# Layer-norm source tiles taken from a resident buffer, and the squares moved from VectorE to ScalarE, in an AdaLN attention and MoE layer on 8 cores

## The reference

```python
mod = (_silu(L0_c) @ L0_wmod).reshape(4, 6, 1, -1)
sa, ca, ga, sb, cb, gb = (mod[:, 0], ..., mod[:, 5])
ga = (2 * (ga >= 0) - 1) * jnp.maximum(jnp.abs(ga), 0.25)   # gb the same
h = _layernorm(x, axis=-1) * (1 + ca) + sa        # x is (4, 2048, 2048)
x = x + ga * attention(h)                         # 16 heads of 128, causal
h = _layernorm(x, axis=-1) * (1 + cb) + sb
x = x + gb * moe(h)                               # 8 experts top 2, one shared
```

## Time and profile before

| | us |
|---|---|
| median of 2 runs | 4139.27 (4135.47 to 4143.06) |
| profiled execution, its own time | 4139.3 |
| span of its slowest core, core 4 | 4137.7 |
| spans of the other cores | 4119.7 to 4132.9 |
| PE busy (core 4) | 3338.9, 81% of the span |
| DVE busy | 1175.2, 28% |
| ACT busy | 596.3, 14% |

### The profile page before, as it was taken

How to read it: one execution, slowest core, us unless ns; L and a number is a source line. 1 busy time by engine, 2 the same in 40 slices (tenths; PEclk the granted TensorE clock), 3 DMA queues, 4 the chain that set the end, 5 groups by cost and what they waited for, 6 DMA issues and landing times. The chain is left out here.

```text
span 4137.7 us, 46112 instructions; the slowest of 8 cores (4119.7 to 4137.7 us)
## 1 busy us (share of the span) xinstructions
PE 3338.9 (81%) x14133; PEld 1368.3 (33%) x14394; DVE 1175.2 (28%) x2063; ACT 596.3 (14%) x1288; POOL 469.5 (11%) x891
## 2 busy tenths in 40 slices
PE   3434388888888878888895289999999999999997
PEld 0222222222222222222233134444444444444443
DVE  0255522222222222222225612132221222212212
ACT  0122222222222222222201200000000000000000
POOL 1101000000000000000000012122122121211211
PEclk9666677777777777777787589999999999999998
DMA  9866511111111111111122035545555454554544
GB/s 206 145 139 143 114 19 16 18 19 17 20 16 16 16 21 16 16 16 16 16 42 35 1 53 86 77 71 77 74 75 81 68 79 70 74 82 69 74 74 117
DMA packets 128926, 246.51 MB, mean 60 GB/s; under 512 B 15681, under 2 KB 56770, under 8 KB 126402
## 3 DMA queue, kind: packets, MB, share of 16 engines
q0 software_dynamic: 125824, 209.92, 33.3%
q1 hardware_dynamic: 2882, 33.63, 2.3%
HBM read 444.94 MB, written 8.39 MB: 110 GB/s over the span
## 5 line engine op out<-in xcount | busy, mean ns | idle before, releaser
L593 PE MATMUL pacc<-h_full,rA 128*128 128x512 bf16 x2497 | 596.9, 395 | 20.7 <-DMA rA<-wk 14.7
L1298 PE MATMUL pdn<-ysb,rD 128*128 128x512 bf16 x2510 | 565.9, 386 | 15.9 <-DVE ysb L1242 11.5
L1188 PE MATMUL px<-h,rA 128*128 128x512 bf16 x2508 | 564.8, 380 | 3.9 <-ACT comb L347 1.2
L1213 PE MATMUL px<-h,rA 128*128 128x512 bf16 x2508 | 562.2, 379 | 2.7
L593 PEld LDWEIGHTS pacc<-h_full,rA 128*128 128x128 bf16 x2560 | 257.1, 101 | 346.4 <-issue 74.9
L1230 DVE TENSOR_TENSOR ysb<-x1s,px 128x1024 bf16<-128x1024 bf16 x80 | 97.7, 1221 | 960.7 <-PE px L1213 960.7
L1298 PEld LDWEIGHTS pdn<-ysb,rD 128*128 128x128 bf16 x2560 | 253.4, 99 | 327.0 <-issue 36.0
L1188 PEld LDWEIGHTS px<-h,rA 128*128 128x128 bf16 x2560 | 251.1, 98 | 305.1 <-issue 4.8
L1213 PEld LDWEIGHTS px<-h,rA 128*128 128x128 bf16 x2560 | 250.4, 98 | 302.1
L1308 DVE SCALAR_TENSOR_TENSOR x_own<-pdn,gbcl,x_own 128x512 f32<-128x512 f32 x320 | 240.2, 751 | 342.0 <-PE pdn L1298 342.0
L1202 ACT ACTIVATE x1s<-px 128x1024 bf16<-128x1024 f32 x80 | 81.8, 1023 | 1479.5 <-PE px L1188 1479.5
(11 more groups left out here) (153 smaller groups left out, 2433.3 us busy)
## 6 DMA issues: line engine op xcount, KB each, us to landing
rB<-wmodA POOLq DMA_DIRECT2D x96, 512.0 KB, 10.6
rA<-wg POOLq DMA_DIRECT2D x128, 256.0 KB, 4.8
rA<-wu POOLq DMA_DIRECT2D x128, 256.0 KB, 5.2
rD<-wd POOLq DMA_DIRECT2D x256, 128.0 KB, 5.5
xl<-ximg SPq DMA_DIRECT2D x16, 1024.0 KB, 10.1
rA<-wk POOLq DMA_DIRECT2D x32, 256.0 KB, 5.0
rA<-wq POOLq DMA_DIRECT2D x32, 256.0 KB, 4.8
rA<-wv POOLq DMA_DIRECT2D x32, 256.0 KB, 4.8
```

The costliest lines, as they stand in the source:

```text
L593: t.matmul(pacc[:, bank * 512:bank * 512 + 512], ub[:, (dc % 8) * 128:(dc % 8) * 128 + 128], moving_fn(dc, qtr), start=(dc == 0), stop=(dc ...
L1188: lambda t, ub=ub, dc=dc, half=half: t.matmul(px1[:, half * 512:half * 512 + 512], ub[:, (dc % 8) * 128:(dc % 8) * 128 + 128], h2[:, dc * ...
L1213: lambda t, ub=ub, dc=dc, half=half: t.matmul(px3[:, half * 512:half * 512 + 512], ub[:, (dc % 8) * 128:(dc % 8) * 128 + 128], h2[:, dc * ...
L1298: t.matmul(pdn[rot][:, :], ub[:, dloc * 128:dloc * 128 + 128], ysb[:, hc * 1024 + th * 512: hc * 1024 + th * 512 + 512], start=(hc == 0), ...
```

## The change

Two edits are in the diff. First, `emit_ln_cast` makes both bf16 copies on ACT, the second as an activation with `Square`; DVE's multiply and its mark `sq_mark` go. As both norms use this helper, it holds for all 16 + 8 pieces. Second, in LN1 pieces with even `s` take their source from `x_own`; only the eight odd chunks are loaded into `xl`. The two tiles `xl` alternate over the odd pieces alone, and `ld_x(s + 2)` is issued at the head of odd piece `s`, waiting for `v_h` of piece `s - 2`. Even pieces wait for `s_xo`, the landing of `x_own`. Lines behind the helper lie five lower than before up to the loader (L421 is L416, L437 is L432).

```diff
-        s_c1 = em.op("scalar", lambda s: s.activation(xbfb[:, :], x_src_ap, AF.Copy),
-                     waits=w_cast, inc=True)
-
-        def _sq(v):
-            with nc.allow_low_precision(reason="bf16 x^2 operand for LN variance stats"):
-                return v.tensor_tensor(xsqb[:, :], x_src_ap, x_src_ap, ALU.mult)
-        v_sq = em.op("vector", _sq, waits=list(w_cast), inc=True)
-        em.drain("vector")
-        state["cast_mark"] = s_c1
-        state["sq_mark"] = v_sq
+        em.op("scalar", lambda s: s.activation(xbfb[:, :], x_src_ap, AF.Copy),
+              waits=w_cast, inc=True)
+        s_c2 = em.op("scalar", lambda s: s.activation(xsqb[:, :], x_src_ap, AF.Square),
+                     inc=True)
+        state["cast_mark"] = s_c2
...
-        w_mm = [state["cast_mark"], state["sq_mark"], misc["CG"]]
+        w_mm = [state["cast_mark"], misc["CG"]]
...
-        slot = s_idx % 2
+        slot = (s_idx // 2) % 2
...
+    x_wait = [None] * TC
+
+    def src_of(s):
+        if s % 2 == 0:
+            return x_own[:, (s // 2) * 2048:(s // 2 + 1) * 2048]
+        return xl[(s // 2) % 2][:, :]
+
     if SUB1 >= 2:
-        xw0 = ld_x(0)
-        emit_ln_cast(xl[0][:, :], xbf[:, :], xsq[:, :], ln1_state,
-                     extra_waits=[xw0])
+        x_wait[1] = ld_x(1)
+        emit_ln_cast(src_of(0), xbf[:, :], xsq[:, :], ln1_state,
+                     extra_waits=[(s_xo, 16)])
     for s_idx in (range(TC) if SUB1 >= 2 else range(0)):
-        slot = s_idx % 2
+        if s_idx % 2 == 1 and s_idx + 2 < TC:
+            x_wait[s_idx + 2] = ld_x(s_idx + 2)
         pc = None
         if s_idx + 1 < TC:
-            xw = ld_x(s_idx + 1)
-            nslot = (s_idx + 1) % 2
-            pc = (lambda xw=xw, nslot=nslot:
-                  emit_ln_cast(xl[nslot][:, :], xbf[:, :], xsq[:, :],
-                               ln1_state, extra_waits=[xw]))
+            nxt = s_idx + 1
+            ew = [(s_xo, 16)] if nxt % 2 == 0 else [x_wait[nxt]]
+            pc = (lambda nxt=nxt, ew=ew:
+                  emit_ln_cast(src_of(nxt), xbf[:, :], xsq[:, :],
+                               ln1_state, extra_waits=ew))
...
-        x_free[slot] = v_h
+        if s_idx % 2 == 1:
+            x_free[(s_idx // 2) % 2] = v_h
```

More of the change, by code:

```diff
@@ L538, in build_nc @@
                   emit_mod_half(mbh // 2, mbh % 2, ringB, pma_h, p_mt[:, :], stage="b"))
-        v_h = emit_ln_piece(xl[slot][:, :], dst, ca1, 0, p_rs[0:1, 0:128],
+        v_h = emit_ln_piece(src_of(s_idx), dst, ca1, 0, p_rs[0:1, 0:128],
                             p_rq[0:1, 0:128], ln1_state, rows_b1, p_bc1[:, :],
```

## The result

| | before | after |
|---|---|---|
| forecast | | 4077, range 4058 to 4102 |
| time | 4139.27 | 4078.9 to 4085.6 |
| ratio to before | | 0.9853 (0.9821 to 0.9884) |
| profiled execution, slowest core | 4137.7 (core 4) | 4084.0 (core 1) |
| LN1, 15 periods, all cores | 323.8 to 336.2 | 258.5 to 258.7 |

The median over all twelve executions after, 4192.66 us, mixes in seven in which a die ran at a lower clock; only the others are compared. The ratio times 4139.27 is 4078.4 us. The means of the executions compared are 4082.7 us after and 4139.1 before, 56 us apart; the ratio comes out lower since it counts one execution of the kernel before that took 4171.6. "LN1" in the table is DVE's first row instruction (L395 before, L390 after) from the first to the last piece, "attention" from the end of LN1 to the start of the third block.

The account below looks back on a forecast made before the run. ACT's wait for late chunks of x was taken to set LN1's pace. LN1 gains 103.8 - 27.2 - 0.9 = 75.7 us, LN2 loses 13.6: 62.1 off 4139.3 gives 4077.2, range 4058 to 4102.

Parts of the forecast that it names:

- Loads, LN1: First layer norm: with resident even chunks and early odd loads no cast waits; gain 102.5 us plus 1.3, 103.8 us.
- Squares, LN1: First layer norm: Square on ACT adds 1.81 us in each of 15 precasts, 27.2 us, plus 0.9 in the first piece.
- Squares, LN2: Second layer norm: only cost, 7 precasts at 1.81 us, 12.7, plus 0.9 for the first; 13.6 us lost.
- Sum: Whole kernel, core 4: 75.7 gained in LN1 less 13.6 lost in LN2, 62.1 us off 4139.3, giving 4077.2.
- the clock term of my range: Attention: a 0.01 shift of TensorE's granted clock, 0.76, moves 1405.7 us of matmul by up to 18 us.
- What is late next: LN1 after the change: DVE stays last in each piece; the statistics on PE end 3.7 us ahead of L395.
- The modulation units: Rival, LN1: units take the place of x and hold the loop, 4085 to 4154 us; chance 0.10.
- The rule on moving work: Both norms: DVE idle while ACT is on the path, so loads alone would be about 41 us better.
- its own opening point: LN1: a late load of chunk s+1 holds up chunk s through ACT's list; ACT waits 102.5 us, 14 times.

Follow-up runs that it names:

- e1: Changed kernel with the squares back on VectorE, so only the loads differ from the kernel before: 4039.6 and 4044.8 us, ratio 0.9779.
- e2: Kernel before with both copies on ScalarE, loads as before: 4172.6 to 4175.1 us, ratio 1.0098.
- e4: Changed kernel with the square on ScalarE, but behind the copy of rows_b: 4038.4 and 4044.1 us.
- e11: Kernel before, loads unchanged, cast on ScalarE moved behind everything the piece needs, square in its old place on VectorE: 4125.2 us beside 4135.1.
- e5: Kernel before, loads unchanged, both copies on ScalarE at the end of its list of the piece: 4037.6 to 4045.9 us, ratio 0.9773.
- e12: Kernel before with one more wait on POOL, holding back the modulation units until the next chunk's tile is free: 4078.2 and 4080.1 us, ratio 0.9844.
- e8: Changed kernel; LN1: square on VectorE, cast on ScalarE behind rows_b; LN2: both on ScalarE behind rows_b: 4024.3 to 4025.5 us, ratio 0.9735.

## Why the prediction was right, and where it was not

*Loads, LN1* was right. The wait of 102.5 us is gone entirely; from 15 periods of 336.2 us, 103.8 off and 27.2 on, I had 259.6 for core 4, and every core measured 258.5 to 258.7. Core 4 was the end of a range: the gain of LN1 was 77.5 us on it and 65.3 to 77.2 on the others, which had waited less. Attention's first matmul on core 4 starts 79.3 us earlier; I had 76.

*Squares, LN1* was right: 1.89 us, a pitch of 1.80 to 1.81, no table load beyond the one that was there. The run with loads alone (e1) puts the whole cost of the squares at about 40 us against 41.7. What the Trainium skill states (ScalarE: Activation LUTs, "What ACT_TABLE_LOAD costs") held for Square: by it 1.89 us and a pitch of 1.80, in this trace 1.89 and 1.80 to 1.81.

*Squares, LN2*: 7 periods grew by 12.6 us (12.7 expected), and the stretch from the start of the third block to the first matmul of the gating from 127.7 to 140.9, 13.2 against 13.6.

*Sum*: core 4 gained 77.5 us in LN1 and lost 12.6 in LN2; but its span fell by 80.1, since its attention was 10.1 us shorter and its first piece began 1.9 earlier (76.9 of the 80.1). Core 1's span fell by 45.0: LN1 77.2 gained, LN2 12.6 lost, attention 10.6 longer, and 9 more in stretches that nothing in the change reaches. The slowest core of an execution is set by this spread as well, and what was gained in all, 61 us by the ratio and 56 by the means, stands between the two. So the two norms came out as summed (64.9 us off on core 4, 62.1 forecast), and that the time did too is in part luck. Attention varied by 16 us between cores of the execution after, with no part of the change in it. On core 4 it is the clock term of my range: it had 1394.7 us of matmul there at a granted clock of 0.77, where before it had 1405.7 at 0.76, for the same 5237 matmuls in the record. What set the clock was not tried.

*What is late next* held in the changed kernel; DVE is last in each piece, and L390 waits for ACT only in the first, where there is no piece before it.

*The modulation units* was the weak step. I took their DMA work as today's 14.6 us a piece less half a load of x, and forecast a share of 0.75. It is 0.85, which is 0.85 x 240.4 / 14 = 14.6 us a piece; the load that went was made up by slower units. The saturated price of 3.25 a unit, which gave 14.9, was the better number. It did no harm at a period of 17.2, where L266 waited for `rB` 0.2 to 17.0 us by core in the whole of LN1 and LN1 took 258.5 to 258.7 on all of them, and it set the pace as soon as the square was off the chain.

*The rule on moving work.* The Trainium skill (Perfetto Trace Analysis, "Optimizing Scalar/DVE Operations") says that offloading to ScalarE may make sense if VectorE is saturated. I stretched this to say that an idle VectorE should keep its work, and in LN2 it was not even idle, with 102.8 us busy of 128. e1 and e2 (+0.98%) seem to bear the stretched rule out, but it is the place in the list and not the engine that decided. LN2 shows it: 104.1 us before, 116.7 with the square ahead of `rows_b` on ScalarE, 104.1 with it behind (e4), 99.8 with the cast alone behind (e11), 98.8 with both behind (e5).

What my account missed is its own opening point. I wrote that a late chunk s+1 holds up chunk s because its cast stands in front in ACT's list (DVE's list holds it as well, e11), and then costed only the cure by earlier loads. e5 shows the other, and e12 a third: 10.0 us of landing were not the load's own, but partly the price of being issued behind two or three units. The forecast was right since the change makes the landing time irrelevant (10.5 to 13.3 us in the median by core, and no wait), not since I understood it.

## What to carry to other kernels

A wait for a load has three cures, and the timeline tells them apart: issue the load earlier, issue it ahead of the bulk traffic that shares the DMA engines, or move its first consumer behind the work of the present step, in every engine's list that has it. The second was one wait here and gained as much as the change under study (ratios 0.9844 and 0.9853), though less than its loads without its squares (0.9779). Before moving an elementwise copy to another engine, ask what stands behind it in that engine's list: 1.8 us in front of `rows_b` cost 1.8 us a piece, behind it nothing (e1 and e4 agree in both norms within 3 us).

## What the runs showed of the hardware that was not expected

- A 1 MB chunk landed in 10.0 us (median) when two or three units of 1 MB read each had been pushed ahead of it, the first by 1.3 to 2.5 us, at a DMA share of 0.64. In the changed kernel, at a share of 0.85, with two ahead of it, the first by 1.4 to 1.5 us, it took 13.3 (core 1). With the units held back by one wait it landed in 6.1; issued 1.5 to 2.6 us ahead of them, but with the DMA share at 1.00, in 7.1 (e5). The issues of e12, 0.47 us apart, and the saturated stretch of e5:

```profile
280.79 0.33 SPq L511 DMA_DIRECT2D xl<-ximg  x1
```

```profile
281.26 2.18 POOL L101 DMA_DIRECT2D rB<-wmodA  x4 [16.18 <-DVE rowb L396]
```

```profile
175.00:375.00 200.00, 106.78 (x639) 65.23 (x639) 130.49 (x266) 87.34 (x163) 25.32 (x48) 0.71 1.00 194
```

- That stretch shows 194 GB/s, against 162 and 164 in the saturated stretch of units alone. This is not more speed: the column counts bytes as they land, and a unit reads twice what it lands (32 units of 0.52 MB in 104 us are 161 GB/s). By bytes read the two are alike, 323 GB/s for units alone and 5.24 MB per 16.1 us, 326, in e5.
- The same transfers take more of the DMA engines' time when packed closer: share times period is 14.6 us for four units and a chunk in the kernel before, and 16.1 in e5; in the changed kernel it is 14.6 with half a chunk. I had reckoned them as fixed.
- The spread between cores in LN1 (323.8 to 336.2 before) came from the wait for x alone: ACT's wait was 90.2 to 102.5 us by core, and LN1 less that wait is 233.6 to 234.0 on every core. In the changed kernel all agree within 0.2 us; where the units set the pace they differ again (219.7 to 230.2 in e8).
